# A graph-and-feed-forward kernel whose first linear layer goes from float32 to pairs of float16

## The chip, the cores and the metric

The kernel runs on one core of one Trainium2 chip. The metric is the device time of one execution in microseconds (us), the median of several executions. In what follows PE is TensorE (matmuls and transposes), DVE is VectorE, ACT is ScalarE, POOL is GpSimd, and SP is the engine that issues the DMAs.

## The reference, cut to what matters

Four layers follow one another on 1250 nodes of 1024 features, each one added to its input: graph attention, a feed-forward layer of small rails, a graph convolution, a layer of experts. Only the first changes.

```python
z = jnp.einsum('ni,hif->nhf', h, W)          # h = layernorm(x), W: 4 heads x 1024 x 256
el = jnp.einsum('nhf,hf->nh', z, a_l)
er = jnp.einsum('nhf,hf->nh', z, a_r)
e = jax.nn.leaky_relu(el[src] + er[dst], NEG_SLOPE)
m = jax.ops.segment_max(e, dst, num_segments=N)
ex = jnp.exp(e - m[dst])
s = jax.ops.segment_sum(ex, dst, num_segments=N)
alpha = ex / s[dst]
out = jax.ops.segment_sum(alpha[:, :, None] * z[src], dst, num_segments=N)
...
x = x + _L0_gnn_ref(_layernorm(x, axis=-1), L0_gnn_W, L0_gnn_a_l, L0_gnn_a_r, src, dst)
```

## The kernel before

The function `opening` does all that comes before attention's softmax. It works on ten tiles of 125 nodes. For each tile it does two unrelated things that share the engines.

**The edge counts.** The 20,000 edges are sorted by target and cut into 160 chunks of 125. For every chunk that meets the tile (16 for the first and last tile, 20 for most) DVE makes two one-hot matrices (`hots`, L298 to L307: `hot_src` 125x1250 and `hot_dst` 125x125) and PE multiplies them into `ps_count` with three matmuls (L440). There are four buffers of each, so DVE can be four chunks ahead of PE and no more. The counts are copied by ACT to `count_f` (L500), cast by POOL and stored, transposed by PE (L454) and copied by ACT to `ct` (L515).

**The linear layer.** DVE takes mean and variance of the rows of x (`stats`), normalises a tile into the one buffer `xn` (L295), PE transposes it in eight pieces into `ps_t` (`turn`, L394), ACT copies it to `xt` (`x_copy`, L472), and PE multiplies it with W, which lies in `wz` (`half_z`, L415: eight float32 matmuls with 512 columns for each half of the 1024 outputs). ACT copies each half to the one buffer `z` (L481), SP stores it, and DVE takes the products with `a_l` and `a_r` (`dots`, L347). `ps_t` is shared: transposed x, transposed counts and, in the first tile, the weights of the rails (`combine`, L404) pass through it.

The order on each engine is the order in which its code is written; nothing plans it. PE, per tile: the count loop, first half of z, transposes of the counts, second half of z, transposes of the next tile's x. DVE, per tile: `hots(t)`, `normalise(t + 1)`, `dots(t - 1)`, `degrees(t - 1)`, with extra work in some tiles: `comb_peaks` in tile 0 (maxima of the rails' combined weights), `comb_scales` in tile 1, `comb_lo` in tile 2 (L332), and the row statistics of x in three groups: tiles 0 and 1, tiles 2 to 5 (in tile 0), tiles 6 to 9 (in tile 3). The last group has a reason to be late. The combined weights of the rails lie where rows 6 to 9 of x will go, so SP loads these rows only after `comb_lo` is done:

```python
                    if t == 2:
                        sp.wait_ge(lo_set, 1)
                        for n in range(LATE, TILES):
                            x_load(n)
```

Of the kernel before, what the change touches and what calls it, by code (L numbers as in the profile page):

```python
# [93 lines left out]
def opening(nc, ident, room, counts, ct, cnt, deg, indeg, X_all, x, w, a_l, a_r, z_d, el, er, src, dst, maker, up, combs, scales, spare, eps):  # L94
# [4 lines left out]
    with ExitStack() as ctx:  # L99
# [20 lines left out]
        wz = c.sb("wz", [128, KT, DIM], F32)  # L120
# [4 lines left out]
        xt = [c.sb(f"xt{k}", [128, KT, P], F32) for k in range(2)]  # L125
        z = c.sb("z", [P, DIM], F32)
# [30 lines left out]
        x_turned, xt_set, z_sum, z_set = c.sem("x_turned"), c.sem("xt_set"), c.sem("z_sum"), c.sem("z_set")  # L157
# [11 lines left out]
        with nc.Block() as block:  # L169

            @block.sync
            def _(sp):
                def x_load(t):
                    rows_to(sp, X[:, t, :], x[t * P:(t + 1) * P, :], x_in[t])

                sp.dma_start(src_i[:], src).then_inc(edges_in, 16)
                sp.dma_start(dst_i[:], dst).then_inc(edges_in, 16)
                sp.dma_start(mk_c, maker.rearrange("(o r) j h i -> (r j) o (h i)", r=8)).then_inc(weights_in, 16)
                sp.dma_start(up_c, up.rearrange("(o r) j h k -> (r j) o (h k)", r=8)).then_inc(weights_in, 16)
                x_load(0)  # L180
                x_load(1)
                for k in range(KT):
                    sp.dma_start(wz[:, k, :], w[k * 128:(k + 1) * 128, :]).then_inc(wz_in[k], 16)
                for n, row in enumerate((a_l, a_r)):
                    sp.dma_start(rows[:, n, :], row.partition_broadcast(128)).then_inc(rows_in, 16)
                for t in range(2, LATE):
                    x_load(t)
                for t in range(TILES):
                    sp.wait_ge(u_ready, t + 1)
                    rows_to(sp, counts[t * P:(t + 1) * P, :], cnt[:, t, :], u_stored)  # L190
                    if t == 2:
                        sp.wait_ge(lo_set, 1)
                        for n in range(LATE, TILES):
                            x_load(n)
                    sp.wait_ge(z_set, 2 * t + 2)
                    rows_to(sp, z_d[t * P:(t + 1) * P, :], z[:], z_stored)
                sp.wait_ge(u_stored, 32 * TILES)
                sp.wait_ge(z_stored, 32 * TILES)

            @block.gpsimd  # L200
            def _(pool):
# [17 lines left out]
                nc.gpsimd.memset(tops[:, OCTETS:OCTETS + 1], TINY).then_inc(tops_set, 1)  # L219
                for t in range(TILES):  # L220
                    if t == 0:
                        pool.wait_ge(comb_sum, OCTETS)
                    pool.wait_ge(f_ready, t + 1)
                    nc.gpsimd.tensor_copy(cnt[:, t, :], count_f).then_inc(u_ready, 1)
                    if t == 0:
                        pool.wait_ge(peaks_set, OCTETS)
                        nc.gpsimd.partition_all_reduce(tops[:, 0:OCTETS], peaks[:], 128, bass.bass_isa.ReduceOp.max).then_inc(tops_set, 1)

            @block.vector
            def _(dve):  # L230
                nc.vector.memset(warm[:], 1.0).then_inc(warm_set, 1)
                nc.vector.memset(eps[:], EPS)
                dve.wait_ge(iotas, 6)
# [102 lines left out]

                def dots(t):
# [18 lines left out]
                for t in range(TILES):  # L356
                    hots(t)
                    if t == 0:
                        stats(0, 0, 2)
                        spread(0, 0, 2)  # L360
                        normalise(0)
                        comb_peaks()
                    if t == 1:
                        spread(1, 2, LATE)
                    if t == 4:
                        spread(2, LATE, TILES)
                    if t + 1 < TILES:
# [7 lines left out]
                    if t == 3:  # L375
# [12 lines left out]
            def _(pe):  # L388
                def turn(t):
                    pe.wait_ge(xn_set, t + 1)  # L390
                    if t >= 1:
                        pe.wait_ge(tu_ready, t)
# [37 lines left out]
                for t in range(TILES):  # L430
# [27 lines left out]
                    if t + 1 < TILES:  # L458
                        turn(t + 1)

            @block.scalar
            def _(act):
                def root(n, lo, hi):
                    act.wait_ge(stat_set, 2 * n + 2)
                    nc.scalar.activation(std[:, lo:hi], mean_var[:, lo:hi, 1], ACT.Sqrt, bias=eps[:]).then_inc(std_set, 1)

                def x_copy(t):
# [3 lines left out]
                    for h in range(2):  # L471
                        cp = nc.scalar.copy(xt[t % 2][:, 4 * h:4 * h + 4, :],  # L472
                                            ps_t[:, h, :].rearrange("p (k f) -> p k f", f=128)[:, :, 0:P])
                    cp.then_inc(xt_set, 1)

                def z_copy(t, half):
# [4 lines left out]
                    nc.scalar.copy(z[:, half * BANK:(half + 1) * BANK], ps_z[:, half, :]).then_inc(z_set, 1)  # L481
# [13 lines left out]
                for t in range(TILES):  # L495
# [12 lines left out]
                    if t == 1:  # L508
                        root(1, 2, LATE)
                    if t == 4:  # L510
# [8 lines left out]
                    if t + 1 < TILES:  # L519
                        x_copy(t + 1)  # L520
# [1806 lines left out]
```

## Time and profile before

| | |
|---|---|
| time, median of 3 executions | 2730.7 us (2727.94 to 2730.82) |
| profiled execution: time | 2728.99 us |
| profiled execution: span | 2727.3 us |
| PE busy | 2578.6 us, 95% of the span |
| DVE busy | 1879.3 us, 69% |
| ACT busy | 1115.4 us, 41% |
| opening (to the first instruction of attention) | 303.95 us |
| first linear layer (L415), 320 PE instructions | 141.4 us of PE busy time |

A row of the timeline gives the start, the length, the engine, the line and operation, output and inputs, shapes and how many instructions are merged; in brackets stands how long the engine was idle before, and who released it. A float32 matmul of the program is two PE instructions in the trace (160 matmuls, 320 rows). Ends of matmuls are modelled and overlap the next start, so paces are read from start to start. "Granted clock" (PEclk) is the share of 2.4 GHz that PE was given; its two levels are 1.00 and 0.50 (1.2 GHz).

### The profile page before, as it was taken

To read this page: it belongs to the slowest core of one execution; us is meant where nothing else is said; L and a number is where in the kernel's file an instruction comes from. 1 tells how busy PE (TensorE), PEld (TensorE's weight loads), DVE (VectorE), ACT (ScalarE), POOL (GpSimd) and SP (SyncE) were. 2 spreads that over 40 slices of the span, in tenths; PEclk is the share of its full clock that TensorE was granted. 3 is DMA by queue.
4 is the path that set the end of the run, shared out by engine and by line. 5 is a ranking of instruction groups with operands and counts; after the bars stand their busy time and mean duration, and the time that the engine had idled before them with its cause. 6 is when DMAs were issued, how large, how long until landed. Compare 5 with 4: busy or idle time off the path is not lost. (4 is left out here: it accounts for less than half of the span.)

```text
span 2727.3 us, 33545 instructions
## 1 busy us (share of the span) xinstructions
PE 2578.6 (95%) x12152; PEld 1700.9 (62%) x12152; DVE 1879.3 (69%) x2340; ACT 1115.4 (41%) x1161; POOL 130.9 (5%) x148
## 2 busy tenths in 40 slices
PE   8999459959999999999999999999999899999998
PEld 5555348846666666666666666666666565575776
DVE  6776768868878887887888788788878543313111
ACT  3211256645554555455455545545552222020111
POOL 0000000010000000000000000000000000000122
PEclk9999779969999999999999999999999899999999
DMA  5200400042232223223222322322240000125996
GB/s 161 62 25 29 95 0 1 1 158 60 54 75 69 60 54 91 53 58 72 69 60 53 91 54 62 67 69 60 53 131 16 14 10 15 41 84 192 300 336 192
DMA packets 172624, 214.56 MB, mean 79 GB/s; under 512 B 66458, under 2 KB 116252, under 8 KB 172490
## 3 DMA queue, kind: packets, MB, share of 16 engines
q1 hardware_dynamic: 166022, 197.24, 26.5%
q0 software_dynamic: 4928, 10.25, 1.5%
q10 hardware_dynamic: 1540, 5.12, 0.5%
q8 instruction: 103, 1.69, 0.3%
q14 instruction: 31, 0.25, 0.0%
HBM read 183.48 MB, written 32.52 MB: 79 GB/s over the span
## 5 line engine op out<-in xcount | busy, mean ns | idle before, releaser
L1455 PE MATMUL rails_ps<-keep_own_w1g,rails_hid_hi 128*125 128x512 f16 x2120 | 632.4, 380 | 2.9 <-issue 2.9
L1455 PE MATMUL rails_ps<-keep_own_w,rails_hid_hi 128*125 128x512 f16 x2080 | 618.7, 379 | 0.0
L1455 PE MATMUL rails_ps<-keep_own_w1g,rails_hid_lo 128*125 128x512 f16 x1060 | 402.5, 380 | 0.0
L1455 PE MATMUL rails_ps<-keep_own_w,rails_hid_lo 128*125 128x512 f16 x1040 | 394.2, 379 | 0.0
L1455 PEld LDWEIGHTS rails_ps<-keep_own_w1g,rails_hid_hi 128*125 128x125 f16 x2120 | 285.4, 137 | 159.8 <-issue 3.4
L1455 PEld LDWEIGHTS rails_ps<-keep_own_w,rails_hid_hi 128*125 128x125 f16 x2080 | 279.7, 137 | 151.3
L1004 ACT ACTIVATE rails_hid_hi<-rails_raw_a,keep_scale_hidden 128x1000 f16<-128x1000 f32 x210 | 274.7, 1336 | 210.1 <-DVE rails_raw_a L1215 97.0
L1196 DVE SCALAR_TENSOR_TENSOR rails_hid_lo<-rails_raw_a,keep_scale_hidden,rails_hid_hi 128x1000 f16<-128x1000 f32 x210 | 312.2, 1517 | 42.0 <-ACT rails_hid_hi L1004 42.0
L994 ACT ACTIVATE rails_raw_a<-rails_ps,keep_scale_gelu 128x1000 f32<-128x1000 f32 (+1 forms) x192 | 182.6, 953 | 347.8 <-PE rails_ps L1440 344.9
L1250 DVE SCALAR_TENSOR_TENSOR keep_X<-rails_ps,rails_out_scale,keep_X 125x1024 f32<-125x1024 f32 x180 | 198.7, 1104 | 144.0 <-PE rails_ps L1455 144.0
L1455 PEld LDWEIGHTS rails_ps<-keep_own_w1g,rails_hid_lo 128*125 128x125 f16 x1060 | 145.0, 137 | 84.6 <-issue 0.8
L1455 PEld LDWEIGHTS rails_ps<-keep_own_w,rails_hid_lo 128*125 128x125 f16 x1040 | 142.0, 136 | 82.5
L757 PE MATMUL att_ps_o<-att_zh,counts_room 125*125 125x257 f32 x800 | 175.8, 383 | 6.2 <-DVE counts_room L666 6.2
L979 ACT ACTIVATE rails_raw_a<-carried_w_land 128x2048 f32<-128x2048 f32 x64 | 121.7, 1902 | 135.4 <-DMA carried_w_land<-cproj 135.4
L757 PEld LDWEIGHTS att_ps_o<-att_zh,counts_room 125*125 125x125 f32 x800 | 150.5, 189 | 31.3 <-issue 6.4
L1250 DVE SCALAR_TENSOR_TENSOR rails_acc<-rails_ps,rails_out_scale,rails_acc 125x1024 f32<-125x1024 f32 x135 | 147.8, 1102 | 31.0 <-PE rails_ps L1455 30.9
L303 DVE TENSOR_SCALAR open_hot_src<-open_iota_h,open_src_f 125x1250 f16<-125x1250 f16 x196 | 106.5, 543 | 74.6 <-PE open_ps_count L440 70.0
L415 PE MATMUL open_ps_z<-open_wz,open_xt 128*125 128x512 f32 x320 | 141.4, 595 | 1.1 <-ACT open_xt L472 1.1
L940 POOL PARTITION_ALL_REDUCE rails_tops<-rails_sums x64 | 50.5, 789 | 1688.4 <-ACT rails_raw_a L979 1688.4
L1204 DVE SCALAR_TENSOR_TENSOR keep_own_w1g<-carried_w_land,rails_w_scale,keep_own_w1g 128x2048 f16<-128x2048 f32 x53 | 124.2, 2343 | 0.1
L1204 DVE SCALAR_TENSOR_TENSOR keep_own_w<-carried_w_land,rails_w_scale,keep_own_w 128x2048 f16<-128x2048 f32 x52 | 121.8, 2343 | 0.0
L1440 PE MATMUL rails_ps<-rails_xs,rails_cm 128*128 128x250 f16 (+1 forms) x768 | 102.9, 259 | 17.4 <-DMA rails_xs<-xt_d 9.9
(358 smaller groups left out, 3446.1 us busy)
## 6 DMA issues: line engine op xcount, KB each, us to landing
carried_w_land<-cproj SPq DMA_DIRECT2D x79, 1024.0 KB
ffn_w<-W SPq DMA_DIRECT2D x51, 1024.0 KB, 12.1
rails_xs<-xt_d SPq DMA_DIRECT2D x128, 78.1 KB, 5.1
xt_d<-rails_acc SPq DMA_DIRECT2D x20, 250.0 KB
keep_X<-x SPq DMA_DIRECT2D x10, 448.0 KB
z_d<-open_z SPq DMA_DIRECT2D x10, 448.0 KB
att_zh<-z_d SPq DMA_DIRECT2D x4, 1120.0 KB
xn_d<-ffn_xn SPq DMA_DIRECT2D x10, 448.0 KB
```

What stands on the lines that cost most here:

```text
L303: nc.vector.tensor_scalar(hot_src[k][:], iota_h[:], src_f[:, bass.ds((first + g) * GROUP + k, 1)], None, ALU.is_equal)
L415: mm = nc.tensor.matmul(ps_z[:, half, :], xt[t % 2][:, k, :], wz[:, k, half * BANK:(half + 1) * BANK], start=(k == 0), stop=(k == KT - 1))
L757: mm = nc.tensor.matmul(ps_o[:, bank(g, d), 0:ZW], wt[m % DEEP][:, d * P:(d + 1) * P], zh[:, h, s, :], start=(s == 0), stop=(s == TILES - 1))
L940: nc.gpsimd.partition_all_reduce(tops[:, TOP[name]:TOP[name] + 1], sums[:, TOP[name]:TOP[name] + 1], 128, bass.bass_isa.ReduceOp.max).then ...
L979: nc.scalar.activation(junk, b_of[name], ACT.Abs, accum_out=sums[:, k:k + 1]).then_inc(summed, 1)
L994: nc.scalar.activation(to, source, ACT.Gelu, scale=scales["gelu"][:, 0:1]).then_inc(gelu_set[name], 1)
L1004: nc.scalar.activation(hid[(q + b) % 2]["hi"][:, :, PIECES[piece]], raw[SOURCE_A[q]][:, :, PIECES[piece]], ACT.Copy, scale=scales["hidden" ...
L1196: nc.vector.scalar_tensor_tensor(part["lo"][:, :, PIECES[piece]], raw[SOURCE_A[q]][:, :, PIECES[piece]], scales["hidden"][:, 0:1], part["h ...
L1204: nc.vector.scalar_tensor_tensor(part["lo"], b_of[SOURCE_W[q]], w_scale[:, k:k + 1].bitcast(F32), part["hi"], ALU.mult, ALU.subtract).then ...
L1250: nc.vector.scalar_tensor_tensor(to, ps[0:P, a:b, :], out_scale[0:P, k:k + 1], to, ALU.mult, ALU.add).then_inc(acc_used, 1)
L1440: mm = nc.tensor.matmul(ps[:, at, col:col + wide], cm[pair][:, h, :], xs[pair][:, half * WN + lo * P:half * WN + hi * P], start=True, stop ...
L1455: mm = nc.tensor.matmul(ps[0:P, t, :], hid[(q + b) % 2][l][:, k, t * P:(t + 1) * P], w[(q + b) % 2][r][:, k, :], start=(k == 0 and i == 0) ...
```

## The change

W is kept as a pair of float16 matrices, high part and rest, and so is the transposed x; the product is three float16 matmuls (high by high, high by low, low by high) where one float32 matmul was. To keep the range, W is scaled by a power of two found from its largest element, x by 256 (through the standard deviation), and the copy of z out of PSUM divides both away.

The buffer `wz` gets a ninth slot: W is loaded into slots 1 to 8 and part k of the pair is written over slot k, which held the raw part k-1. The program's constant `SPLIT`, and the same method, are in use already in the later layers (L1455, L1803).

```diff
+        w_part = [{n: wz[:, k, i * BANK:(i + 1) * BANK].bitcast(F16) for i, n in enumerate(("hi", "lo"))} for k in range(KT)]
...
-        xt = [c.sb(f"xt{k}", [128, KT, P], F32) for k in range(2)]
-        z = c.sb("z", [P, DIM], F32)
+        xt = [{n: c.sb(f"xt_{n}{k}", [128, KT, P], F16) for n in ("hi", "lo")} for k in range(2)]
+        z = spare[0][0:P, 0:DIM]
...
+                pool.wait_ge(w_peaks_set, KT)
+                nc.gpsimd.partition_all_reduce(w_tops[:, 0:KT], w_peaks[:], 128, bass.bass_isa.ReduceOp.max).then_inc(w_tops_set, 1)
                 for t in range(TILES):
...
+                def w_maxima():
+                    for k in range(KT):
+                        dve.wait_ge(wz_in[k], 16)
+                        nc.vector.tensor_reduce(w_peaks[:, k:k + 1], wz[:, k + 1, :], AX.X, ALU.max,
+                                                apply_absolute_value=True).then_inc(w_peaks_set, 1)
+                def w_scales():
...
+                def w_lo():
+                    for k in range(KT):
+                        dve.wait_ge(w_hi_set, k + 1)
+                        nc.vector.scalar_tensor_tensor(w_part[k]["lo"], wz[:, k + 1, :], w_up[:, 0:1].bitcast(F32), w_part[k]["hi"],
+                                                       ALU.mult, ALU.subtract).then_inc(w_lo_set, 1)
+                def x_lo(t):
+                    dve.wait_ge(xt_hi_set, t + 1)
+                    for h in range(2):
+                        sub = nc.vector.tensor_tensor(xt[t % 2]["lo"][:, 4 * h:4 * h + 4, :],
+                                                      ps_t[:, h, :].rearrange("p (k f) -> p k f", f=128)[:, :, 0:P],
+                                                      xt[t % 2]["hi"][:, 4 * h:4 * h + 4, :], ALU.subtract)
+                    sub.then_inc(xt_lo_set, 1)
...
                     if t == 0:
                         stats(0, 0, 2)
+                        w_maxima()
                         spread(0, 0, 2)
                         normalise(0)
+                        w_scales()
                         comb_peaks()
-                    if t == 1:
+                        x_lo(0)
+                        normalise(1)
+                        w_lo()
+                        stats(1, 2, LATE)
                         spread(1, 2, LATE)
-                    if t == 4:
+                    if t + 1 < TILES:
+                        x_lo(t + 1)
+                    if t == 3:
                         spread(2, LATE, TILES)
-                    if t + 1 < TILES:
-                        normalise(t + 1)
-                    if t == 0:
-                        stats(1, 2, LATE)
+                    if t + 2 < TILES:
+                        normalise(t + 2)
                     if t == 1:
                         comb_scales()
                     if t == 2:
                         comb_lo()
-                    if t == 3:
                         stats(2, LATE, TILES)
...
                         if t == 0:
-                            pe.wait_ge(wz_in[k], 16)
-                        mm = nc.tensor.matmul(ps_z[:, half, :], xt[t % 2][:, k, :], wz[:, k, half * BANK:(half + 1) * BANK],
-                                              start=(k == 0), stop=(k == KT - 1))
+                            pe.wait_ge(w_lo_set, k + 1)
+                        for n, (l, r) in enumerate(SPLIT):
+                            mm = nc.tensor.matmul(ps_z[:, half, :], xt[t % 2][l][:, k, :], w_part[k][r][:, half * BANK:(half + 1) * BANK],
+                                                  start=(k == 0 and n == 0), stop=(k == KT - 1 and n == 2))
...
-                    pe.wait_ge(xt_set, t + 1)
+                    if t + 1 < TILES:
+                        turn(t + 1)
+                    pe.wait_ge(xt_lo_set, t + 1)
                     half_z(t, 0)
                     pe.wait_ge(f_ready, t + 1)
+                    pe.wait_ge(xt_lo_set, min(t + 2, TILES))
                     for j in range(TILES):
...
                     half_z(t, 1)
-                    if t + 1 < TILES:
-                        turn(t + 1)
...
+                def w_hi():
+                    act.wait_ge(w_scale_set, 1)
+                    for k in range(KT):
+                        if k >= 1:
+                            act.wait_ge(w_lo_set, k)
+                        nc.scalar.activation(w_part[k]["hi"], wz[:, k + 1, :], ACT.Copy,
+                                             scale=w_up[:, 0:1].bitcast(F32)).then_inc(w_hi_set, 1)
...
                         x_copy(0)
-                    if t == 1:
+                        w_hi()
                         root(1, 2, LATE)
-                    if t == 4:
+                    if t + 1 < TILES:
+                        x_copy(t + 1)
+                    if t == 3:
                         root(2, LATE, TILES)
                     z_copy(t, 0)
```

DVE in tile 0, before: after the maxima of the combined weights (L312) come the next tile's normalisation and the statistics of tiles 2 to 5.

```order
L284 BN_AGGR open_mean_var<-open_stat 125x2
L289 RECIPROCAL open_rstd<-open_std 125x2 [waits open_std_set]
L295 TENSOR_SCALAR open_xn<-keep_X,open_mean_var,open_rstd 125x1024 [waits open_rstd_set]
...
L295 TENSOR_SCALAR open_xn<-keep_X,open_mean_var,open_rstd 125x1024 [waits open_x_turned]
L81 BN_STATS open_stat<-keep_X 125x6 [waits open_x_in2]
```

The same stretch after: L352 takes the maxima of W's eight parts (the first and last stand here), L369 writes its eight low parts, L375 the low part of x.

```order
L296 BN_AGGR open_mean_var<-open_stat 125x2
L352 TENSOR_REDUCE open_w_peaks<-open_wz 128x1 [waits open_wz_in0]
...
L352 TENSOR_REDUCE open_w_peaks<-open_wz 128x1 [waits open_wz_in7]
L301 RECIPROCAL open_rstd<-open_std 125x2 [waits open_std_set]
L307 TENSOR_SCALAR open_xn<-keep_X,open_mean_var,open_rstd 125x1024 [waits open_rstd_set]
...
L324 TENSOR_REDUCE open_peaks<-keep_X 128x1 [waits open_comb_set] x8
L375 TENSOR_TENSOR open_xt_lo<-open_ps_t,open_xt_hi 128x500 [waits open_xt_hi_set]
L375 TENSOR_TENSOR open_xt_lo<-open_ps_t,open_xt_hi 128x500
L307 TENSOR_SCALAR open_xn<-keep_X,open_mean_var,open_rstd 125x1024 [waits open_x_turned]
L369 SCALAR_TENSOR_TENSOR open_wz<-open_wz,open_w_up 128x1024 [waits open_w_hi_set] x8
L81 BN_STATS open_stat<-keep_X 125x6 [waits open_x_in2]
```

All of W's work stands between the statistics of tiles 0 and 1 and those of tiles 2 to 5, ahead of `x_lo(1)`.

DVE in tile 2, before: from `comb_lo` (L332) it goes straight on to the products of tile 1 (L347).

```order
L295 TENSOR_SCALAR open_xn<-keep_X,open_mean_var,open_rstd 125x1024 [waits open_x_turned]
L332 SCALAR_TENSOR_TENSOR early_comb_lo<-keep_X,open_up_scale,early_comb_hi 128x4096 [waits open_hi_set]
L347 ISA keep_own_w,keep_el<-open_z,open_rows 125x256 [waits open_z_set,open_dots_set]
L347 ISA keep_el 125x1
L347 ISA keep_own_w,keep_er<-open_z,open_rows 125x256
```

After (`comb_lo` is L344, the products L390):

```order
L375 TENSOR_TENSOR open_xt_lo<-open_ps_t,open_xt_hi 128x500 [waits open_xt_hi_set]
L375 TENSOR_TENSOR open_xt_lo<-open_ps_t,open_xt_hi 128x500
L307 TENSOR_SCALAR open_xn<-keep_X,open_mean_var,open_rstd 125x1024 [waits open_x_turned]
L344 SCALAR_TENSOR_TENSOR early_comb_lo<-keep_X,open_up_scale,early_comb_hi 128x4096 [waits open_hi_set]
L81 BN_STATS open_stat<-keep_X 125x6 [waits open_x_in6]
...
L81 BN_STATS open_stat<-keep_X 125x6 [waits open_x_in9]
L81 BN_STATS open_stat<-keep_X 125x6
L296 BN_AGGR open_mean_var<-open_stat 125x2 [waits open_stat_set]
L296 BN_AGGR open_mean_var<-open_stat 125x2 x3
L390 ISA keep_own_w,keep_el<-keep_own_w1g,open_rows 125x256 [waits open_z_set,open_dots_set]
```

The statistics of tiles 6 to 9 moved from tile 3 to here, one instruction behind the one that lets SP load them.

## Rows read from the trace of the kernel before

**Rows 1.** Timeline of PE over one tile: start, length, line, operands, count.

```profile
88.91 7.11 PE L415 MATMUL open_ps_z<-open_wz,open_xt 128*125 128x512 f32 x16
95.86 1.25 PE L454 MATMUL open_ps_t<-keep_ident,open_iota_i 125*125 125x125 f32 x10
96.95 7.03 PE L415 MATMUL open_ps_z<-open_wz,open_xt 128*125 128x512 f32 x16
103.82 1.02 PE L394 MATMUL open_ps_t<-keep_ident,open_xn 125*128 125x125 f32 x8
...
105.20 11.62 PE L440 MATMUL open_ps_count<-open_hot_src,open_hot_dst 125*125 125x512 f16 x60
...
116.80 7.11 PE L415 MATMUL open_ps_z<-open_wz,open_xt 128*125 128x512 f32 x16
```

**Rows 2.** Timeline of PE in the rails layer, ten float16 trios apart.

```profile
2115.99 0.59 PE L1502 MATMUL rails_ps<-keep_own_w1g,rails_hid_hi 128*125 128x512 f16 x2
...
2122.46 0.59 PE L1502 MATMUL rails_ps<-keep_own_w1g,rails_hid_hi 128*125 128x512 f16 x2
```

**Rows 3.** Timeline of the last count loop, DVE and PE.

```profile
275.98 0.55 DVE L303 TENSOR_SCALAR open_hot_src<-open_iota_h,open_src_f 125x1250 f16<-125x1250 f16 x1 [9.56 <-PE open_ps_count L440]
...
283.39 0.42 DVE L347 CUSTOM_DVE_ANT_0 keep_own_w<-open_z,open_rows 125x256 bf16<-125x256 f32 x1
...
284.11 0.28 PE L444 MATMUL open_ps_count<-open_iota_h,open_zeros_h 125*125 125x1 f16 x3
...
286.15 1.45 DVE L353 TENSOR_REDUCE open_deg_part<-counts_room 125x10 f32<-125x1250 uint16 x1
```

**Rows 4.** Timeline of ACT and PE at the end of count loop 1.

```profile
60.86 0.28 PE L444 MATMUL open_ps_count<-open_iota_h,open_zeros_h 125*125 125x1 f16 x3
...
62.38 0.29 ACT L465 ACTIVATE open_std<-open_mean_var,keep_eps 125x4 f32<-125x4 f32 x1
```

**Rows 5.** Groups by line and form, whole span: busy us, mean ns of one.

```profile
L472 ACT COPY open_xt<-open_ps_t 128x500 f32<-128x500 f32 x20 | 10.5, 579 | 3.6 <-PE open_ps_t L394 3.6
...
L1660 DVE TENSOR_TENSOR graph_xt_lo<-graph_ps_x,graph_xt_hi 128x500 f16<-128x500 f32 x20 | 12.6, 672 | 6.1 <-ACT graph_xt_hi L1605 6.0
...
L1044 ACT ACTIVATE carried_w_land<-rails_raw_a,carried_w_up 128x1024 f16<-128x1024 f32 x4 | 4.3, 1133 | 0.0
```

**Rows 6.** Timeline of DVE where the graph layer's W is measured and split.

```profile
2090.61 4.59 DVE L1256 TENSOR_REDUCE rails_next_peaks<-rails_raw_a 128x1 f32<-128x1024 f32 x4
...
2138.01 2.48 DVE L1287 SCALAR_TENSOR_TENSOR carried_w_land<-early_comb_hi,carried_w_up,carried_w_land 128x1024 f16<-128x1024 f32 x2 [1.28 <-ACT carried_w_land L1044]
```

**Rows 7.** Timeline of tile 0 on DVE, with POOL's reduction.

```profile
24.45 0.28 DVE L284 BATCH_NORM_AGGREGATE open_mean_var<-open_stat 125x2 f32<-125x12 f32 x2
...
26.59 0.17 DVE L289 RECIPROCAL open_rstd<-open_std 125x2 f32<-125x2 f32 x1 [1.86 <-ACT open_std L465]
...
27.52 4.83 DVE L312 TENSOR_REDUCE open_peaks<-keep_X 128x1 f32<-128x512 f32 x8
...
32.26 0.80 DVE L295 TENSOR_SCALAR open_xn<-keep_X,open_mean_var,open_rstd 125x1024 f32<-125x1024 f32 x1
32.98 4.83 DVE L81 BATCH_NORM_STATS2 open_stat<-keep_X 125x6 f32<-125x512 f32 x8
...
37.08 0.40 POOL L227 PARTITION_ALL_REDUCE open_tops<-open_peaks  x1 [5.58 <-issue]
```

**Rows 8.** Timeline of tile 2: `comb_lo`, and the first late load of x.

```profile
88.76 4.48 DVE L332 SCALAR_TENSOR_TENSOR early_comb_lo<-keep_X,open_up_scale,early_comb_hi 128x4096 f16<-128x4096 f32 x1
...
95.48 0.34 SPq L90 DMA_DIRECT2D keep_X<-x  x1
```

**Rows 9.** Windows: busy us per engine, granted clock, DMA share, GB/s.

```profile
14.00:16.00 2.00, 2.00 (x10) 1.32 (x9) 1.89 (x7) 2.00 (x4) 0.00 (x0) 1.00 1.03 412
...
95.50:104.30 8.80, 8.80 (x33) 4.65 (x32) 5.36 (x19) 2.10 (x5) 0.00 (x0) 1.00 0.94 255
```

**Rows 10.** Window after an idle stretch of PE, same columns.

```profile
303.00:308.50 5.50, 4.51 (x22) 4.55 (x23) 1.06 (x4) 2.89 (x6) 0.17 (x1) 0.50 0.58 151
```

More of the change, by code:

```diff
@@ L156, in opening @@
         stat_set, std_set, rstd_set, xn_set = c.sem("stat_set"), c.sem("std_set"), c.sem("rstd_set"), c.sem("xn_set")
-        x_turned, xt_set, z_sum, z_set = c.sem("x_turned"), c.sem("xt_set"), c.sem("z_sum"), c.sem("z_set")
+        x_turned, xt_hi_set, xt_lo_set = c.sem("x_turned"), c.sem("xt_hi_set"), c.sem("xt_lo_set")
+        z_sum, z_set = c.sem("z_sum"), c.sem("z_set")
+        w_peaks_set, w_tops_set, w_step, w_scale_set = [c.sem(n) for n in ("w_peaks_set", "w_tops_set", "w_step", "w_scale_set")]
+        w_hi_set, w_lo_set = c.sem("w_hi_set"), c.sem("w_lo_set")
         z_stored, dots_set = c.sem("z_stored"), c.sem("dots_set")
@@ L335, in comb_lo @@
                                                    ALU.subtract).then_inc(lo_set, 1)
+                def w_maxima():
[4 more added lines that the diff above has]
+                def w_scales():
+                    dve.wait_ge(w_tops_set, 2)
+                    nc.vector.tensor_reduce(w_peak[:], w_tops[:], AX.X, ALU.max).then_inc(w_step, 1)
+                    dve.wait_ge(w_step, 1)
+                    nc.vector.tensor_scalar(w_two[:], w_peak[:].bitcast(I32), EXPONENT, None, ALU.bitwise_and).then_inc(w_step, 1)
+                    dve.wait_ge(w_step, 2)
+                    nc.vector.tensor_scalar(w_down[:], w_two[:].bitcast(F32), 2.0 ** -W_UP / XN_UP, None, ALU.mult)
+                    nc.vector.tensor_scalar(w_up[:], w_two[:], -1.0, float(INVERT + (W_UP << 23)), ALU.mult,
+                                            ALU.add).then_inc(w_scale_set, 1)
+                def w_lo():
[10 more added lines that the diff above has]
+                    sub.then_inc(xt_lo_set, 1)
                 def dots(t):
@@ L391, in turn @@
                     if t >= 1:
[L392 removed]
+                        pe.wait_ge(xt_lo_set, t)
+                    if t >= 2:
+                        pe.wait_ge(tu_ready, t - 1)
                     for k in range(KT):
@@ L464, in root @@
                     act.wait_ge(stat_set, 2 * n + 2)
-                    nc.scalar.activation(std[:, lo:hi], mean_var[:, lo:hi, 1], ACT.Sqrt, bias=eps[:]).then_inc(std_set, 1)
+                    nc.scalar.activation(std[:, lo:hi], mean_var[:, lo:hi, 1], ACT.Sqrt, bias=eps_up[:],
+                                         scale=1.0 / XN_UP ** 2).then_inc(std_set, 1)
+                def w_hi():
[5 more added lines that the diff above has]
+                                             scale=w_up[:, 0:1].bitcast(F32)).then_inc(w_hi_set, 1)
                 def x_copy(t):
@@ L471, in x_copy @@
                     for h in range(2):
-                        cp = nc.scalar.copy(xt[t % 2][:, 4 * h:4 * h + 4, :],
+                        cp = nc.scalar.copy(xt[t % 2]["hi"][:, 4 * h:4 * h + 4, :],
                                             ps_t[:, h, :].rearrange("p (k f) -> p k f", f=128)[:, :, 0:P])
-                    cp.then_inc(xt_set, 1)
+                    cp.then_inc(xt_hi_set, 1)
                 def z_copy(t, half):
@@ L480, in z_copy @@
                         act.wait_ge(dots_set, t)
-                    nc.scalar.copy(z[:, half * BANK:(half + 1) * BANK], ps_z[:, half, :]).then_inc(z_set, 1)
+                    nc.scalar.activation(z[:, half * BANK:(half + 1) * BANK], ps_z[:, half, :], ACT.Copy,
+                                         scale=w_down[0:P, 0:1]).then_inc(z_set, 1)
                 act.wait_ge(warm_set, 1)
```

14 lines of the change are left out of this document (9 added, 5 removed).

## The prediction

> **What bounds the kernel now.** I read the timeline of PE first, over one tile of the opening. PE never rests there: half of z from 88.91, transposes of the counts from 95.86, the other half from 96.95, transposes of x from 103.82, the count loop from 105.20, and the next tile's z at 116.80 [rows 1]. So a tile of 20 chunks takes 116.80 - 88.91 = 27.9 us, of which the linear layer holds (95.86 - 88.91) + (103.82 - 96.95) = 6.95 + 6.87 us. Then DVE. In the count loop it delivers a chunk every (283.39 - 275.98) / 12 = 0.617 us, and had waited 9.56 us for PE before it [rows 3]. PE is the bound outside the loop; inside, DVE sets the pace and its four chunks of lead only shorten the start. What counts for the change is therefore (a) PE's time outside the loop, and (b) whether DVE has its four chunks ready when PE comes. The rest of the program, from 303.95 on, is untouched; the sum is made on the opening of the profiled execution (span 2727.3 us, executed in 2728.99) and its difference is carried over to the median, 2730.7.
>
> I use one mark per tile, the end of its count loop: 60.86 for tile 1 [rows 4] and 284.11 for tile 9 [rows 3].
>
> **Part 1: the matmuls (gain).** Eight float32 matmuls of a half take 6.87 us. Ten float16 trios with 512 columns start 2122.46 - 2115.99 = 6.47 us apart, 0.647 a trio [rows 2]; a half has eight: 5.18. The gain is 1.69 a half, 3.38 a tile. Tile 0 is treated apart, so 9 x 3.38 = **-30.4 us**, if PE stays the bound outside the loop.
>
> Does it? Walk one tile after the change, from the mark (0). PE: transposes of x(t+1) from 0.15 to 1.0, half 1 to 6.25, transposes of counts (96.95 - 95.86 = 1.09) to 7.35, half 2 to 12.5, start of the next loop 0.53 later (105.20 - 103.82 less 0.85 for the transposes), at 13.05. DVE: ACT begins its copy of the counts at once and is free 62.38 - 60.86 = 1.52 after the mark [rows 4]; its two copies of x take 1.05 (579 ns each, overlapping), to 2.6; the two subtractions of `x_lo` cost 0.60 each (busy 12.6 us for 20) to 3.85 [rows 5]; normalisation 0.72 (32.26 to 32.98) to 4.55 [rows 7]; `dots` 286.15 - 283.39 = 2.76 to 7.3 and `degrees` 1.4 to 8.7 [rows 3]; four chunks to 11.2. PE arrives at 13.05 and its loop takes the 11.5 us it takes now. Were DVE without any lead, the mark would come 20 x 0.617 + (284.11 - 283.39) = 13.05 after its first chunk began, at 21.75. PE's 24.5 is later by 2.75 us, so PE sets the period, which falls from 27.9 to 24.5. The copy of z, now with a scale, the copy's f16 output and the store of z lie in ACT's and SP's idle time. What is late next is DVE, once those 2.75 us are used up.
>
> **Part 2: measuring and splitting W (loss).** All of it is in DVE's row before tile 1's work, and for the first time PE waits for it: the second half of tile 0 needs `xt_lo(1)`, which stands behind. DVE's clock, from the end of the first statistics at 24.45 + 0.28 = 24.7 [rows 7]:
> - eight maxima of 128x1024: four took 4.59 us [rows 6], so 9.0, to 33.7;
> - reciprocal and `normalise(0)`: 27.52 - 26.59 = 0.93, to 34.65. POOL's reduction is quick (0.40); the 5.58 us of "issue" before it [rows 7] stood after its cast, is issued before the wait now and lies in POOL's idle time from 4.5 us on; if it came after the maxima instead, it would add 5;
> - the four small scale operations 0.6; the eight maxima of the combined weights 32.26 - 27.52 = 4.74 [rows 7], to 40.0;
> - `x_lo(0)` 1.2 and `normalise(1)` 0.72, to 41.9;
> - the low parts. `w_lo(0)` 1.24 to 1.28 (2.48 us for two) [rows 6]. From here the two engines alternate: `w_hi(k)` waits for `w_lo(k-1)`, since it writes over the raw part that this one reads. ACT's half costs 1.13 [rows 5], two hand-overs some 0.05 each, so 2.5 us a part: 43.2 + 7 x 2.5 = 60.8. No row shows such an alternation; side by side the parts would cost 1.24 each (8.8 less), with hand-overs of 0.15 they cost 1.4 more. I take 2.5, as the wait is in the code;
> - statistics of tiles 2 to 5: 4.83, and their aggregation 0.5 (two took 0.28) [rows 7], to 66.1; root and `x_copy(1)` on ACT 1.35, `x_lo(1)` 1.25, to 68.8.
>
> PE then does the transposes of the counts (1.1) and the second half (5.2), to 75.1, and reaches the loop at 75.6. DVE's chunks are ready.
>
> The clock: PE has been idle or nearly so since 61.6. After such a stretch PE ran at 0.50, the 1.2 GHz level, through 303.0 to 308.5 while it was busy for 4.51 us [rows 10]. Work that is done at half clock for 4.6 us gives up 2.3 us; between 0 and 2.5 I take 2.3. The Trainium skill (TensorE: Matmul & The Clock Gate, section "What's actually happening") says that the default state is throttled and activity releases it. By that rule a stretch that starts after idling always begins at half clock, as in this row; without it the final time would be 2.3 us less.
>
> Loop at 77.9, end of count 1 at 77.9 + 11.5 = 89.4, against 60.86: **+28.5 us** (bounds 26 and 31, and 33 with POOL's 5).
>
> **Part 3: the statistics of tiles 6 to 9, one tile earlier (loss).** In tile 2 DVE runs, from the mark: `x_lo(3)` to 3.85, `normalise(4)` to 4.55, `comb_lo` 4.4 (4.48 us) [rows 8] to 8.95. Only now does SP load x for tiles 6 to 9, and DVE's next instruction waits for it; behind it on DVE stand `dots(1)`, `degrees(1)` and the one-hots of tile 3, for which PE waits. Before, this load was issued at 95.48 [rows 8] and moved about 2.2 MB with the counts' store at 255 GB/s until 104.30, with the queues 0.94 busy [rows 9]: 8.8 us. The 2.0 MB alone take 7.8 at that pace, and 4.9 at the 412 GB/s seen once in tile 0 [rows 9], where other loads ran. I take 8.8, the same load, with 4.9 and 10 (1.2 more, for landing) as its bounds: 17.75. The last tile's two statistics and the aggregation 1.7, `dots` and `degrees` 4.15: 23.65. The 20 chunks come with no lead, 13.05 as above: 36.7. Without the stall it is 24.5. PE's clock falls again meanwhile, but it can lag three chunks and nearly catch up: +0.4. Together **+12.6 us** (8.7 to 13.8). What covered this load before was the whole count loop of tile 3.
>
> **Sum.** 28.5 + 12.6 - 30.4 = +10.7; 2730.7 + 10.7 = **2741.4 us**.
>
> **The rivals.**
> - *DVE becomes the bound* (chance 0.08). Its reserve is 2.75 us a tile. POOL's cast runs next to `x_lo`, and more hand-overs stand in DVE's chain than before. Were DVE later by 4.2 us, the period would be 26.0 in eight tiles, +12: 2753. Against it: each price but the hand-overs is a row of the same operation, and a load of its own that size is not in the tile.
> - *The stalls are short* (0.17). With the load at 412 GB/s (3.9 less) and a clock that stays up (2.3 less) the sum is 10.7 - 6.2 = +4.5: 2735, no difference that can be measured. For it: the queues carried the counts' store as well in that window [rows 9]. Against it: the 412 was not this load.
> - *W's work is hidden* (0.05), the one that ends faster. If maxima and low parts fell into time in which DVE waits anyway, 9.0 + 17.6 us go and the sum is -16: 2715. It is faster by 0.2% from the point at which part 2 costs less than 12.3 us. For it: DVE waits much in the opening, 9.56 us before one loop alone [rows 3]. Against it: those waits lie in later tiles, and W is needed in tile 0, where the chain above has no such gap.
>
> **How the numbers follow.** My forecast holds 0.70: slower, between 26 + 8.7 - 30.4 = +4 and 31 + 13.8 - 30.4 = +14. The range goes a little beyond, halfway to the rivals on both sides: 2733 to 2751. About 0.2% (5.5 us) is what a measurement of this kernel tells from no change. Slower by more than that: 0.70 + 0.08 = 0.78; within: 0.17; faster: 0.05.
>
> **What would show it.** In the profile after: float16 trios of the first layer 0.65 us apart; a period of 24.5 us from tile 4 on, with DVE waiting for PE before the fifth chunk (else the first rival); low parts of W 2.5 us apart, with each engine idle between; the end of count 1 near 89 us; in tile 2 a wait of DVE on the DMA of x, 7 to 9 us, and a PE gap of some 12 us with the clock at 0.50 after it; attention's first instruction near 314 us against 303.95. If attention begins before 304, part 2 is wrong; if the end of count 1 is right but the later periods are not 24.5, part 1 is.

## The result, and the profile after

The changed kernel takes **2742.4 us** (2741.64 to 2744.83, five executions) against 2730.7 (also the median of five, 2727.94 to 2730.82); the ratio is 1.0048, with a 95% interval of 1.0037 to 1.0060. It is slower, by the amount and in the places that were forecast, though one of the three terms was too small by 2.3 us.

The page of the changed kernel, its first parts:

```profile
span 2741.1 us, 33926 instructions
## 1 busy us (share of the span) xinstructions
PE 2557.8 (93%) x12312; PEld 1711.6 (62%) x12312; DVE 1906.6 (70%) x2381; ACT 1125.0 (41%) x1169; POOL 128.5 (5%) x150
...
PEclk7999869978999999999999999999999999999999
```

The span is longer, and neither of the other two lines tells why. PE's share is 93% and every engine has idle time; only the clock's first digits hint at the opening. The reading has to go by place, so I begin with the marks of the prediction, the end of each tile's count loop (the row of L444 before, L494 after; us from the span's start). Two rows of the changed kernel stand for them all:

```profile
89.35 0.28 PE L494 MATMUL open_ps_count<-open_iota_h,open_zeros_h 125*125 125x1 f16 x3
...
316.77 0.17 POOL L624 MEMSET att_zh<- 125x40 f32 x1 [13.33 <-POOLq L177]
```

| mark | before | after | difference |
|---|---|---|---|
| tile 1 | 60.86 | 89.35 | +28.49 |
| tile 2 | 88.76 | 113.84 | +25.1 |
| tile 3 | 116.66 | 153.22 | +36.6 |
| tile 4 | | 177.71 | |
| tile 9 | 284.11 | 300.24 | +16.13 |
| attention's first instruction | 303.95 | 316.77 | +12.82 |

The account can be read off. Tile 0 costs 28.49. The eight periods up to tile 9 bring 16.13 - 28.49 = -12.36; one of them, tile 3's, lasts 39.38 instead of the 24.49 of its neighbours, +14.9. Without that excess the eight would bring 27.3, 3.41 each. The tail after the last mark gives 3.31. Together 28.5 + 14.9 - 30.6 = +12.8. (The span grew by 13.8, the medians by 11.7.)

**The saving**, PE's timeline after the fifth mark (202.19), to be laid beside [rows 1]:

```profile
203.22 0.60 PE L465 MATMUL open_ps_z<-open_wz,open_xt_hi 128*125 128x512 f16 x2
203.65 0.38 PE L465 MATMUL open_ps_z<-open_wz,open_xt_lo 128*125 128x512 f16 x1
203.87 0.59 PE L465 MATMUL open_ps_z<-open_wz,open_xt_hi 128*125 128x512 f16 x2
...
208.40 1.25 PE L507 MATMUL open_ps_t<-keep_ident,open_iota_i 125*125 125x125 f32 x10
209.49 0.60 PE L465 MATMUL open_ps_z<-open_wz,open_xt_hi 128*125 128x512 f16 x2
```

Trios start 0.65 apart and a half lasts 208.40 - 203.22 = 5.18 instead of 6.95. No row of PE in this tile has an idle time in brackets: it is still the bound.

**Tile 0**, DVE's timeline after its first statistics (compare [rows 7]):

```profile
24.72 9.05 DVE L352 TENSOR_REDUCE open_w_peaks<-open_wz 128x1 f32<-128x1024 f32 x8
...
35.28 4.83 DVE L324 TENSOR_REDUCE open_peaks<-keep_X 128x1 f32<-128x512 f32 x8
40.03 1.25 DVE L375 TENSOR_TENSOR open_xt_lo<-open_ps_t,open_xt_hi 128x500 f16<-128x500 f32 x2
...
41.91 1.28 DVE L369 SCALAR_TENSOR_TENSOR open_wz<-open_wz,open_w_up 128x1024 f16<-128x1024 f32 x1
44.42 1.28 DVE L369 SCALAR_TENSOR_TENSOR open_wz<-open_wz,open_w_up 128x1024 f16<-128x1024 f32 x1 [1.22 <-ACT open_wz L524]
...
59.42 1.28 DVE L369 SCALAR_TENSOR_TENSOR open_wz<-open_wz,open_w_up 128x1024 f16<-128x1024 f32 x1 [1.22 <-ACT open_wz L524]
60.62 4.84 DVE L81 BATCH_NORM_STATS2 open_stat<-keep_X 125x6 f32<-125x512 f32 x8
```

Between two low parts DVE is idle for 1.22 us in 2.50, and what ends the wait is ACT. ACT's row is its mirror image:

```profile
43.23 1.15 ACT L524 ACTIVATE open_wz<-open_wz,open_w_up 128x1024 f16<-128x1024 f32 x1 [4.36 <-DVE open_wz L369]
45.74 1.15 ACT L524 ACTIVATE open_wz<-open_wz,open_w_up 128x1024 f16<-128x1024 f32 x1 [1.35 <-DVE open_wz L369]
```

PE meanwhile waits for the low part of x(1), and starts at half clock. PE's timeline, and then three windows (busy us and instructions of PE, PEld, DVE, ACT, POOL; granted clock; share of the DMA queues; GB/s):

```profile
68.70 2.43 PE L507 MATMUL open_ps_t<-keep_ident,open_iota_i 125*125 125x125 f32 x10 [6.41 <-DVE open_xt_lo L375]
...
70.93 1.06 PE L465 MATMUL open_ps_z<-open_wz,open_xt_hi 128*125 128x512 f16 x2
```
```profile
70.00:72.00 2.00, 2.00 (x9) 1.61 (x9) 2.00 (x7) 0.83 (x2) 0.00 (x0) 0.50 0.00 0
72.00:74.00 2.00, 2.00 (x7) 1.06 (x7) 0.27 (x2) 0.50 (x2) 0.00 (x0) 0.63 0.00 0
74.00:76.00 2.00, 2.00 (x11) 1.28 (x10) 0.00 (x0) 0.00 (x0) 0.00 (x0) 1.00 0.00 0
```

The same pair of matmuls shows 1.06 us here and 0.60 after the fifth mark.

**Tile 2**, DVE from `comb_lo` to the one-hots of tile 3, with SP's first issue of the load, and PE:

```profile
118.34 4.48 DVE L344 SCALAR_TENSOR_TENSOR early_comb_lo<-keep_X,open_up_scale,early_comb_hi 128x4096 f16<-128x4096 f32 x1
122.85 0.32 SPq L90 DMA_DIRECT2D keep_X<-x  x1
127.22 1.29 DVE L81 BATCH_NORM_STATS2 open_stat<-keep_X 125x6 f32<-125x512 f32 x2 [4.39 <-DMA keep_X<-x]
...
132.81 1.29 DVE L81 BATCH_NORM_STATS2 open_stat<-keep_X 125x6 f32<-125x512 f32 x2 [0.51 <-DMA keep_X<-x]
...
138.56 0.54 DVE L315 TENSOR_SCALAR open_hot_src<-open_iota_h,open_src_f 125x1250 f16<-125x1250 f16 x1
...
142.85 0.55 DVE L315 TENSOR_SCALAR open_hot_src<-open_iota_h,open_src_f 125x1250 f16<-125x1250 f16 x1 [0.33 <-PE open_ps_count L490]
```
```profile
139.31 14.07 PE L490 MATMUL open_ps_count<-open_hot_src,open_hot_dst 125*125 125x512 f16 x60 [12.29 <-DVE open_hot_dst L317]
```

The load was issued at 122.85 and the last tile's statistics began at 132.81, 9.96 us later. DVE's four waits for it (4.39, 0.57, 0.65 and 0.51) add up to 6.1 us only, since the statistics of one tile run while the next lands. (The prediction had named 7 to 9 us of waiting as a sign; its sum went by the landing of the last tile, which such overlap does not shorten.) The last DVE line is worth a look: DVE makes one-hots for a PE at half clock and finds all its chunk buffers full.

### The profile page after: what moved, and what is told of

Same layout as the page of the kernel before. It is cut to its first block and busy times, and to the rows that moved or that the text cites. A ratio compares the mean times of both kernels' runs of the same rounds, so it can differ in the third digit from the quotient of the medians.

```text
span 2741.1 us, 33926 instructions
## 1 busy us (share of the span) xinstructions
PE 2557.8 (93%) x12312; PEld 1711.6 (62%) x12312; DVE 1906.6 (70%) x2381; ACT 1125.0 (41%) x1169; POOL 128.5 (5%) x150
## 5 line engine op out<-in xcount | busy, mean ns | idle before, releaser
L490 PE MATMUL open_ps_count<-open_hot_src,open_hot_dst 125*125 125x512 f16 (+1 forms) x588 | 117.7, 357 | 12.3 <-DVE open_hot_dst L317 12.3
```

Of the source, the lines that this page charges most:

```text
L490: mm = nc.tensor.matmul(ps_count[:, a:b], hot_dst[k][:], hot_src[k][:, a:b], start=False, stop=False)
```

## The experiments

They are numbered; "run 4" is the fourth of them. Totals are medians beside runs of the kernel before on the same chip. Single terms I take from the marks in the traces.

**1. Statistics put back.** The statistics of tiles 6 to 9, their root and reciprocal go one tile later again, where they stood before; all else as changed.

```diff
                     if t == 2:
                         comb_lo()
+                    if t == 3:
                         stats(2, LATE, TILES)
...
```

> One part undone: the statistics of tiles 6 to 9 (with their root and reciprocal one tile later) stand in tile 3 again, as before the change; all else is as changed. Theory (the vector engine waits for the load that its own previous instruction let loose): the 14.9 us that tile 2 is longer than the others go. In their place the two tiles with extra vector work go beyond PE's 24.5: tile 2 with the low parts of the combined weights alone 8.7 + 4.4 + 13.05 = 26.15 (+1.65), tile 3 with the statistics 8.7 + 5.3 + 13.05 = 27.05 (+2.55). Sum -10.7: 2731.7 us, no wait of DVE on a DMA, no clock of 0.50 after tile 2. Rival (the work on DVE is the cost, the load is hidden): tile 2 loses only the 5.3 us of the statistics and tile 3 gets them, 2740 to 2742 us.

Measured 2731.86 us (ratio to before 1.0007, 0.9997 to 1.0017), marks at 89.35, 113.83, 139.92 and 166.78. Tile 3's period is 26.09 instead of 39.38, tile 4's 26.86. The statistics stand in tile 3 and wait for nothing:

```profile
144.42 4.83 DVE L81 BATCH_NORM_STATS2 open_stat<-keep_X 125x6 f32<-125x512 f32 x8
```

The move cost 11.0 us (316.77 - 305.81 at attention's start); not the whole 14.9, because `comb_lo` and the statistics still lengthen their tiles, by 1.60 and 2.37, standing behind `normalise`. That price shows the reserve at work: 4.48 us put into a tile lengthen it by 1.6, so 2.9 of it lay in time that DVE had to spare.

**2. A second spare slot for W.** The buffer gets two extra slots, so that `w_hi(k)` waits for `w_lo(k-2)` and the engines need not take turns. The low parts of x move into another buffer to make room.

```diff
-        wz = c.sb("wz", [128, KT + 1, DIM], F32)
+        wz = c.sb("wz", [128, KT + 2, DIM], F32)
...
-                        if k >= 1:
-                            act.wait_ge(w_lo_set, k)
+                        if k >= 2:
+                            act.wait_ge(w_lo_set, k - 1)
```

> One cause taken away: W's buffer has two spare slots in place of one, so the high part k waits for the low part k-2 and not k-1, and ACT can be one part ahead; the low parts of x lie in another buffer of the same kind to make room. Theory (the alternation of ACT and DVE costs 1.22 us a part): the low parts start 1.2 to 1.3 us apart in place of 2.50, the last ends near 52 and not 60.7, the end of count loop 1 comes 8.6 us earlier, near 80.8: 2733.8 us. Rival (PE or something behind W sets the end of tile 0): low parts closer together but the end of count loop 1 moves by less than 3 us, 2740 us or more.

Measured 2732.89 us (1.0011, 1.0002 to 1.0021). The eight low parts are one row now, without a wait:

```profile
42.65 9.97 DVE L370 SCALAR_TENSOR_TENSOR open_wz<-open_wz,open_w_up 128x1024 f16<-128x1024 f32 x8
```

They end at 52.55 against 60.62, and the first mark stands at 81.11 against 89.35. From the first low part to the end of the last it is 9.90 us instead of 18.71: 8.8 us of tile 0's 28.5 were the turn-taking and not the arithmetic. Only 8.2 arrive at the mark, since tile 0's count loop ended 0.74 later here (23.49 against 22.75).

**3. Both.**

> Both edits of the two runs before at once. Theory (the two losses lie in different tiles and have nothing to do with each other): the gains add up, -10.7 - 8.6 = -19.3: 2723.1 us, faster than the kernel before the change by 7.6. Rival (a shorter tile 0 only moves the wait on, for instance to the z copies or the stores): less than -15, 2727 us or more.

Measured 2722.2 us (0.9973, 0.9961 to 0.9984): faster than the kernel before. The marks fall at 79.97, 104.45, 130.53 and 157.39, attention begins at 296.41, 20.4 earlier. The gains of 1 and 2 at the same place, 10.96 and 8.05, are 1.35 short of that, and the marks and rows account for it. Tile 0's count loop ended at 23.49 in run 2 and at 22.84 in run 3, which passes on 0.64 to `x_lo(1)`. From there to the first mark run 2 took 21.90 and run 3 21.40, since PE came off the half clock sooner: in run 3, where the transposes began at 59.98, the granted clock of 63 to 64 us is 0.79; in run 2, where they began at 60.62, it is 0.50 until 65. And tile 3 took 39.59 in run 2, 0.21 more than in the changed kernel. The two causes are separate.

**4. PE kept busy.** Matmuls of zeros fill PE's two gaps, 20 before the transposes of the counts in tile 0 and 54 before the count loop of tile 3. They add nothing to any result; the waits stay.

```diff
+                    if t == 0:
+                        for _ in range(20):
+                            nc.tensor.matmul(ps_count[:, 0:BANK], zeros_h[:], iota_h[:, 0:BANK], start=True, stop=True)
                     pe.wait_ge(xt_lo_set, min(t + 2, TILES))
...
```

> The changed kernel with matmuls of zeros added where PE would wait: 20 of 512 columns before the transposes of tile 0's counts, 54 before the count loop of tile 3; they change no result. Theory (part of both losses is work at half clock after idling: 2.4 us in tile 0, 1.6 us in tile 3): granted clock 1.00 when the transposes of tile 0 and the count loop of tile 3 start, -4.0: 2738.4 us. Rival (the clock costs nothing on the path, since DVE sets the pace there): 2742.4 us or more, by what the added matmuls overrun.

```profile
62.08 6.79 PE L510 MATMUL open_ps_count<-open_iota_h,open_zeros_h 125*125 125x512 f16 x20
68.70 1.25 PE L513 MATMUL open_ps_t<-keep_ident,open_iota_i 125*125 125x125 f32 x10
69.79 0.60 PE L465 MATMUL open_ps_z<-open_wz,open_xt_hi 128*125 128x512 f16 x2
```

The transposes start at the same 68.70, but take half as long, and the first mark is 86.95: the clock cost 2.40 in tile 0. Tile 3's period falls from 39.38 to 37.90. DVE's first one-hot comes 0.13 later after the mark than in the changed kernel (24.85 against 24.72), and from there to the next mark it is 13.05 instead of 14.66, so the clock cost 1.6 there. Attention begins 3.90 earlier. In medians it is 2740.17 (1.0037, 1.0023 to 1.0051), 2.2 less than the changed kernel. The medians alone would not show the term: this interval and the changed kernel's overlap, and the program from attention on, which both share, took 2425.0 in one profiled execution and 2424.3 in the other. The marks show it.

**5. DVE's work spread.** On top of the second spare slot of run 2; run 1's move is replaced by this one. No work is left out, but it is put where DVE waits anyway: the maxima of the combined weights after `normalise(2)`; two tiles' statistics instead of four in tile 0; the other statistics and `comb_lo` ahead of an `x_lo`.

```diff
                         w_scales()
-                        comb_peaks()
+                        stats(1, 2, 4)
                         x_lo(0)
                         normalise(1)
                         w_lo()
-                        stats(1, 2, LATE)
-                        spread(1, 2, LATE)
+                        spread(1, 2, 4)
+                    if t == 1:
+                        stats(2, 4, LATE)
+                    if t == 2:
+                        comb_lo()
+                    if 3 <= t <= 6:
+                        stats(t, t + 3, t + 4)
                     if t + 1 < TILES:
                         x_lo(t + 1)
...
                     if t + 2 < TILES:
                         normalise(t + 2)
+                    if t == 0:
+                        comb_peaks()
                     if t == 1:
                         comb_scales()
-                    if t == 2:
-                        comb_lo()
-                        stats(2, LATE, TILES)
...
```

> On top of the wider buffer of W (high part two slots ahead of the raw part), DVE's new work is put where DVE waits anyway: the maxima of the combined weights move from tile 0's chain to the stretch after normalise(2), where DVE waited 5.83 us for PE before its fifth chunk; only two of the four tiles' statistics stay in tile 0, in the gap before x_lo(0); the others, and comb_lo, stand ahead of an x_lo, where DVE waited 3.23 us for ACT's copy. Nothing is left out. My theory (what the change costs is the order of DVE's row in three places, not its amount of work): x_lo(0) at 38.0 instead of 40.1, low parts to 50.0, x_lo(1) at 51.3, PE without a cold start, end of count 1 at about 71.9 against 79.97 with both repairs alone; every later period of 20 chunks 24.5, that is 1.6 and 2.4 less in tiles 2 and 3. Together -12.1: 2710.1 us (2707 to 2713), attention's first instruction near 284.3. Rival (DVE's amount of work is the limit): what leaves tile 0 comes back as longer periods in tiles 1 to 6, and the time stays within 4 us of 2722.

Measured **2706.81 us** (2706.0 to 2708.67; 0.9917, 0.9904 to 0.9931): 0.8% faster than before. The marks are 70.66, 95.20, 119.67 and 144.21, every period of 20 chunks 24.5, and attention begins at 283.14. The first mark is 1.2 earlier than worked out, though the execution was 1.0 late by the end of tile 0's count loop (23.75). Half of these 2.2 us is that I had let `x_lo(1)` wait 1.3 us for ACT, and it began 0.19 after the low parts' end; 0.9 is that from its start to the mark it took 19.74 and not the 20.6 that I had put. One tile's DVE row shows where the statistics went:

```profile
118.96 1.27 DVE L81 BATCH_NORM_STATS2 open_stat<-keep_X 125x6 f32<-125x512 f32 x2
...
122.27 1.26 DVE L376 TENSOR_TENSOR keep_own_w1g<-open_ps_t,open_xt_hi 128x500 f16<-128x500 f32 x2 [1.80 <-ACT open_xt_hi L539]
```

In the changed kernel the wait for ACT at this place is 3.23. Now 1.4 of it is work, and `x_lo` starts no later. The rival, by which DVE's amount of work is the limit, fell: everything gained here came from order and buffers. But my theory went too far in putting all of the cost down to order. Against the kernel before, the first mark still stands 9.8 later (70.66 against 60.86), and the maxima and the low parts of W still stand on tile 0's chain. The kernel before has little to win by such moves: between the end of tile 0's count loop (22.67) and its first mark PE waited only 0.68 and 1.14 us.

**6. One product of three.** From tile 4 on two of the three products are left out, to see where DVE takes over.

```diff
-                        for n, (l, r) in enumerate(SPLIT):
+                        for n, (l, r) in enumerate(SPLIT[:3 if t < 4 else 1]):
...
```

> Leaves out two of the three products of the first linear layer from tile 4 on (high by low and low by high); DVE still makes the low parts. It asks where DVE becomes the bound. PE's own path per tile falls by 32 matmuls of 0.216 us, 6.9 us, from 24.5 to 17.6. My theory: DVE's row takes over at 21.75 us a tile of 20 chunks (8.7 us of other work, then 13.05 for chunks without a lead), so the marks of tiles 5, 7 and 8 come 21.75 apart, DVE no longer waits for PE in the count loop, and PE waits for DVE. The marks of tiles 5 to 9 save 5 x 2.75 = 13.7 and the tail up to 6.9: about 2722 us (2720 to 2730). Rival (DVE has next to no reserve, hand-overs fill it): the period stays above 23.5 and the time above 2732. Rival (DVE has more than I counted): 17.6 to 20, and a time below 2712.

```profile
203.60 1.32 PE L507 MATMUL open_ps_t<-keep_ident,open_iota_i 125*125 125x125 f32 x10 [1.08 <-DVE open_xt_lo L375]
204.77 1.89 PE L465 MATMUL open_ps_z<-open_wz,open_xt_hi 128*125 128x512 f16 x8
...
208.99 15.56 PE L490 MATMUL open_ps_count<-open_hot_src,open_hot_dst 125*125 125x512 f16 x72 [1.80 <-DVE open_hot_dst L317]
```

Columns as in the timelines above; the stretch follows the fifth mark. PE waits for DVE before the loop. The periods of tiles 5, 7 and 8 are 21.69, 21.68 and 21.71, where the prediction's walk through DVE's row gave 21.75: the reserve of 2.75 us is real, and taking two thirds of the matmuls away brings 2.8 a tile, not 6.9. Its only execution took 2722.28 us.

**7. Short maxima.** The maxima of W read 8 columns instead of 1024, so most of the measuring of W is left out.

```diff
-                        nc.vector.tensor_reduce(w_peaks[:, k:k + 1], wz[:, k + 1, :], AX.X, ALU.max,
+                        nc.vector.tensor_reduce(w_peaks[:, k:k + 1], wz[:, k + 1, 0:8], AX.X, ALU.max,
```

> Leaves out most of the measuring of W: each of the eight maxima reads 8 columns instead of 1024, all else as in the changed kernel. It prices the maxima on the chain of tile 0. Taken alone they go from 9.05 us to about 0.9. Theory: they are on the path, but something else is late next. The transposes of x(0) on PE wait for the eight copies of the combined weights, which end near 31.0, so x_lo(0) can't start before 31.1 + 1.9 + 1.1 = 34.2, against 40.03 in the changed kernel: -5.8 us. End of count 1 at 83.5 instead of 89.35, the later periods unchanged, 2736.6 us (2734 to 2739). Rival (nothing stands behind them): the full 8.1, end of count 1 at 81.2, 2734.3. Rival (POOL's library load, 5.58 us in the kernel before, was hidden by the maxima): it shows in part, and the gain is under 4 us.

Measured 2735.95 us (1.0022, 1.0013 to 1.0031), first mark at 83.50. That is the mark worked out, partly by luck: tile 0's count loop ended 0.8 late here (23.54). Of the 8.5 us taken from the maxima (9.05 to 0.58) 5.85 come back, 6.6 with that start allowed for. DVE now waits where it had not, for ACT's root and then for the transposed x:

```profile
25.51 0.58 DVE L352 TENSOR_REDUCE open_w_peaks<-open_wz 128x1 f32<-128x8 f32 x8
27.45 0.17 DVE L301 RECIPROCAL open_rstd<-open_std 125x2 f32<-125x2 f32 x1 [1.36 <-ACT open_std L516]
...
33.94 1.26 DVE L375 TENSOR_TENSOR open_xt_lo<-open_ps_t,open_xt_hi 128x500 f16<-128x500 f32 x2 [0.22 <-ACT open_xt_hi L532]
```

It also tells of POOL's 5.58 us [rows 7]. Its reduction ran at 26.23, at once after the last maximum, with no such stretch ahead of it. So it was not the maxima that covered it. POOL was idle from 4.5 us on in both kernels, which leaves room for it, as the prediction had it; no row shows it there, or says what it is.

## The prediction against the runs

**Part 1, the matmuls: right.** -30.6 against -30.4, 24.49 a tile against 24.5. Runs 1 and 6 show DVE's reserve from both sides, so the first rival had no room: it needed more than 2.8 us of delay on DVE in every tile (2.9 by run 1, 2.8 by run 6).

**Part 2, tile 0: right, step by step.** The maxima end at 33.69 (33.7), `w_lo` begins at 41.91 (41.9) and ends at 60.62 (60.8), the count loop begins at 77.90 (77.9), the mark is 89.35 (89.4). The 2.5 us a part, the one price that no row showed, was read out of the code's waits, and run 2 confirms it: without them a part takes 1.24. Both stretches after PE's long waits began at 0.50, as the prediction had read from [rows 10], and the clock's 2.3 measured 2.40 in run 4. The third rival, hidden work, would have needed gaps in DVE's row between the first statistics and the low parts; from 24.72 to 41.91 there is none over 0.1 us.

**Part 3, the moved statistics: the mechanism right, the size too small, 12.6 against 14.9.** Two terms of it were mis-sized.
- The landing: 8.8 predicted, 9.96 measured. It is not that the queues were slower. The windows of the load:

```profile
122.90:124.00 1.10, 1.10 (x7) 0.70 (x6) 0.00 (x0) 0.00 (x0) 0.00 (x0) 1.00 0.37 41
124.00:126.00 2.00, 2.00 (x11) 1.28 (x10) 0.00 (x0) 0.00 (x0) 0.00 (x0) 1.00 0.88 268
126.00:128.00 2.00, 1.02 (x6) 0.44 (x4) 0.78 (x2) 0.00 (x0) 0.00 (x0) 1.00 1.07 274
...
130.00:132.00 2.00, 0.00 (x0) 0.00 (x0) 1.35 (x3) 0.00 (x0) 0.00 (x0) 0.87 0.75 193
132.00:133.00 1.00, 0.00 (x0) 0.00 (x0) 0.49 (x2) 0.00 (x0) 0.00 (x0) 0.50 0.00 0
```

  In the middle it moved 266 to 274 GB/s, more than the 255 of [rows 9]. But it moved 41 GB/s in the first 1.1 us, and nothing in the last 0.8, before DVE went on. The window of [rows 9] held neither end. It opened on the first bytes of the counts' store, which SP had issued 0.8 us before (94.69), so that the load's own start lay under the store's bytes; and it closed with 2.24 of the 2.36 MB of both moved, before anything that waited for them went on. The bound of 10, which had 1.2 added for landing, was the better value. The Trainium skill (DMA: Bandwidth & Descriptors, section "Anatomy of one DMA — SWDGE (gpsimd) path") gives a transfer a fixed share of about 2 us besides its bytes, most of it after the last byte. It says so of the other issue path; the 1.1 + 0.8 us at the ends of this load of eight DMAs, issued by SP, come to the same size, but with the larger part at the front.
- The clock: 0.4 predicted. From its first one-hot to the mark the loop of tile 3 took 153.22 - 138.56 = 14.66 against 13.05, and run 4 gives the 1.6 back. The granted clock, in windows of the loop (columns as above):

```profile
144.00:145.00 1.00, 1.00 (x5) 0.61 (x4) 0.66 (x3) 0.00 (x0) 0.00 (x0) 0.50 0.00 0
145.00:146.00 1.00, 1.00 (x7) 0.76 (x6) 0.96 (x3) 0.00 (x0) 0.00 (x0) 0.93 0.00 0
```

  I had let PE fall behind by up to three chunks and nearly catch up. It can't fall further behind than DVE's buffers allow: DVE's chunks, else 0.617 apart, are 0.78, 1.05, 1.04, 1.05 and 0.76 apart from 141.02 on, 1.6 us in all, and DVE is what sets this loop's end.

**The sum** of the marks was +12.8 where I had +10.7, and the medians gave +11.7, between the two; that the total came nearer than its third term is luck of about 1 us. The second rival, short stalls, fell with these two terms, each of which came out on the long side. Its 2735 lay inside my range, whose lower end, 2733, was therefore set too low to tell the two apart; the rule that I gave for it, halfway to the rivals, does not lead to 2733.

## What to carry to other kernels

When a cheaper operation needs its operand prepared, look for the engine that prepares it and ask what stands behind that work in its row: here the matmuls gave 30.6 us, and preparing them, with the reordering that came along, took 43.4, of which a buffer slot, a move by one tile and DVE's own waits as hiding places returned 33.6. An in-place split by two engines takes turns unless there is a second free slot (2.50 us a part against 1.24 here), and the price of that can be read from the waits in the code before anything runs. A load's time read from a window that opens on another transfer's bytes and closes with the last ones lacks both of its ends.

## What the runs showed of the hardware

- A half clock on one engine reaches the other through the buffers between them. In tile 3 PE ran its loop at 0.50 until about 145, and the mark came 1.6 us late, not because PE had too much to do (its loop takes 11.5 us at full clock, DVE's chunks 12.3) but because DVE stood still with four full buffers.
- In the changed kernel PE worked on single trios from 44 to 62 us; the clock rose at about 46 and did not hold, from 50 on it was 0.50 again. In run 5, with the parts of W twice as dense, it held (windows with PE alone: busy time, granted clock, share of the queues, GB/s; first of the changed kernel, then of run 5):

```profile
46.00:48.00 2.00, 0.80 (x3) 0.96 0.00 0
48.00:50.00 2.00, 0.86 (x3) 0.89 0.00 0
50.00:52.00 2.00, 1.24 (x3) 0.50 0.00 0
```
```profile
46.00:48.00 2.00, 1.56 (x6) 1.00 0.00 0
48.00:50.00 2.00, 1.22 (x6) 1.00 0.00 0
50.00:52.00 2.00, 1.39 (x6) 1.00 0.00 0
52.00:54.00 2.00, 1.67 (x13) 1.00 0.00 0
```

  The transposes of the counts then take 1.32 us instead of 2.43. So run 5 got back the clock's 2.4 us without a single filler. The denser parts alone did not do it: run 2 has them too, and its clock was 1.00 from 48 to 58, but PE then waited 7.08 us for the low part of x(1), the clock fell in 58 to 60 (0.56), and the transposes took 2.43 again. In run 5 that wait is 0.60.
- Undisturbed periods of 20 chunks lie between 24.47 and 24.54 us in all kernels that keep the three products. At that steadiness one profile settles a term of 1 us, which medians whose executions lie 2.6 to 5.6 us apart can't. What does vary is the time up to the first mark's chain: tile 0's count loop ended between 22.67 and 23.75. In run 2 (23.49) DVE found its buffers full twice in that loop, at 15.94 and 16.98, 0.33 us each time, in the changed kernel (22.75) once, for 0.23, while PE made 4 to 6 matmuls a us instead of the later 7 or 8. That is the blocking of tile 3 again; why PE is slow there stays open, for the granted clock of these windows reads 1.00. A term is better read as a difference of two marks than as a time from the start.
